# Attention over pairs of short batches: probabilities times values as four 256-column matmuls in place of three of 512

## The reference, cut to what matters

```python
qg = q.reshape(b, HKV, G, s, HD)                      # 8 groups of 4 heads
scores = jnp.einsum('bkgqd,bksd->bkgqs', qg, k) / math.sqrt(HD)
attn = jax.nn.softmax(scores + bias[None], axis=-1)    # causal, with a slope per head
out = jnp.einsum('bkgqs,bksd->bkgqd', attn, v)         # <- this product
out = out.reshape(b, H, s, HD).transpose(0, 2, 1, 3).reshape(b, s, H * HD)
```

## Time and profile before

| | |
|---|---|
| median of 3 runs | 2405.1 us (2403.43 to 2405.45) |
| the profiled execution's own time | 2406.15 us |
| its span | 2404.4 us |
| TensorE clock granted, mean | 0.999 of full |
| PE busy | 2378.0 us of the span, 11706 matmuls |
| DVE busy | 1725.5 us, 2770 instructions |
| ACT busy | 1325.7 us, 3273 instructions |
| HBM traffic | 131 GB/s over the span |

### The profile page before, as it was taken

One profiled execution on the slowest core, in us unless ns is written; L12 is line 12 of the kernel. 1 busy time (PEld: TensorE's weight loads), 2 busy tenths in 40 slices (PEclk: granted clock), 3 DMA queues, 4 the chain that ended last, 5 costly groups with the idle time before them and its releaser, 6 DMA issues.

```text
span 2404.4 us, 32917 instructions
## 1 busy us (share of the span) xinstructions
PE 2378.0 (99%) x11706; PEld 1979.4 (82%) x11706; DVE 1725.5 (72%) x2770; ACT 1325.7 (55%) x3273; POOL 246.3 (10%) x272
## 2 busy tenths in 40 slices
PE   8999999999999999999999999999999999999998
PEld 6887788888888888888888888888888888888887
DVE  6758878687836867777855777777874686868682
ACT  4245656566625656566724656565743565747561
POOL 0101010101101001010011101010111101010111
PEclk9999999999999999999999999999999999999999
DMA  7774544341542242423443242423254242423260
GB/s 252 261 288 150 171 140 149 134 155 57 191 142 88 85 140 77 141 79 130 135 157 114 71 158 71 158 71 123 88 177 140 71 150 79 140 89 127 69 208 36
DMA packets 88438, 316.15 MB, mean 131 GB/s; under 512 B 12716, under 2 KB 13228, under 8 KB 87124
## 3 DMA queue, kind: packets, MB, share of 16 engines
q1 hardware_dynamic: 70292, 247.14, 31.0%
q10 hardware_dynamic: 10944, 37.54, 4.2%
q0 software_dynamic: 7040, 29.36, 3.4%
HBM read 282.54 MB, written 31.46 MB: 131 GB/s over the span
## 4 chain that ended last, share of the span: by engine, by line
PE 94%; DVE 2%; DMA 2%; issue 1%; ACT 0%; ACTq 0%; POOL 0%; POOLq 0%; DVEq 0%
PE main L1008 80%; PE pv_bank L1202 3%; PE qt_bank L1167 3%; PE s_bank L1183 2%; PE s_bank L1184 2%; PE pt_bank L1191 1%; PE pt_bank L1008 1%; PE s_bank L1008 1%; PE qt_bank L1008 1%; DMA sums<-in_wo 1%; DVE ring L1483 1%; DMA t_scratch<-sums 1%; DVE setup L1483 0%; PE qt_bank L1104 0%; PE s_bank L1104 0%
## 5 line engine op out<-in xcount | busy, mean ns | idle before, releaser
L1008 PE MATMUL main<-ring,act_hi 128*128 128x512 f32 x3584 | 1147.9, 401 | 0.0
L1008 PEld LDWEIGHTS main<-ring,act_hi 128*128 128x128 f32 x3584 | 641.3, 189 | 111.2
L1008 PE MATMUL main<-ring,act_lo 128*128 128x512 f32 x1792 | 702.1, 392 | 0.0
L1008 PE MATMUL main<-ring,lefts 128*128 128x512 f32 x2688 | 624.5, 391 | 0.0
L1483 DVE TENSOR_TENSOR ring<-raw,ring 128x1024 fp32r<-128x1024 f32 x448 | 555.4, 1242 | 58.7 <-ACT ring L1213 57.1
L1008 PEld LDWEIGHTS main<-ring,lefts 128*128 128x128 f32 x2688 | 501.7, 188 | 103.1
L1213 ACT ACTIVATE ring<-raw 128x1024 fp32r<-128x1024 f32 x448 | 472.4, 1057 | 178.3 <-PE main L1008 165.8
L1008 PEld LDWEIGHTS main<-ring,act_lo 128*128 128x128 f32 x1792 | 336.5, 188 | 74.5
L1810 POOL TENSOR_TENSOR rstd<-mean,half 128x4 f32<-128x4 f32 (+1 forms) x192 | 173.9, 906 | 1617.9 <-DVE mean L1599 1617.9
L1369 ACT ACTIVATE prob<-score,peak 128x64 f32<-128x64 f32 x512 | 136.8, 338 | 159.7 <-DVE peak L1654 159.2
L1341 ACT ACTIVATE sq<-main 128x128 f32<-128x128 f32 x640 | 168.8, 277 | 73.3 <-PE main L1008 69.0
(11 more groups left out here) (146 smaller groups left out, 2353.6 us busy)
## 6 DMA issues: line engine op xcount, KB each, us to landing
raw<-in_wq SPq DMA_DIRECT2D x128, 512.0 KB, 4.0
raw<-t_scratch SPq DMA_DIRECT2D x128, 512.0 KB, 3.3
raw<-in_wo SPq DMA_DIRECT2D x96, 512.0 KB, 3.3
raw<-in_wkv SPq DMA_DIRECT2D x64, 512.0 KB, 3.9
sums<-in_wo ACTq DMA_DIRECT2D x32, 512.0 KB, 6.9
t_scratch<-sums ACTq DMA_DIRECT2D x32, 512.0 KB, 5.0
raw<-f_scratch SPq DMA_DIRECT2D x32, 512.0 KB, 5.4
acc<-in_x POOLq DMA_DIRECT2D x16, 512.0 KB, 3.6
```

The costliest lines, as they stand in the source:

```text
L1008: mm = eng.matmul(bank, a, b, start=start and n == 0 and m == 0, stop=stop and n == len(terms) - 1 and m == 2, skip_group_check=further)
```

## The change

The values are held in one tensor `values` in place of `v_hi` and `v_lo`, with the same bytes. For batch b it has the hi part on that batch's 64 partitions and the lo part on the other 64. `pt_hi` gets the batch's hi probabilities on both halves of the partitions, by a new ScalarE stage `p_twice` of two copies, directly behind `p_hi`. A matmul of `values` by `pt_hi` then sums hi x hi and lo x hi over the 128 rows, and one by `pt_lo`, still zero on the other half, adds hi x lo. Each covers one batch's 256 columns. To place the halves, `v_hi` becomes two copies and `v_lo` two subtractions of 64 partitions each, and `v_lo` crosses the halves.

```diff
         def transpose_p():
             self.fill("pt", "prob_t", (k,), "p_lo")
             self.at(base, when("tp_hi"), lambda: self.add("p_hi", k))
+            self.at(base, when("tp_hi"), lambda: self.add("p_twice", k))
             self.at(base, when("tp_lo"), lambda: self.add("p_lo", k))
...
-        v_hi = sb("v_hi", [P, TILES, 2, HD], F32R)
-        v_lo = sb("v_lo", [P, TILES, 2, HD], F32R)
+        values = sb("values", [P, TILES, 2, BPT, HD], F32R)
...
                 elif stage == "pv":
-                    w.wait_ge("p_hi", k)
+                    w.wait_ge("p_twice", k)
...
-                    for m, (a, p) in enumerate(((v_hi, pt_hi), (v_hi, pt_lo), (v_lo, pt_hi))):
-                        mm = eng.matmul(pv_bank[:, :, :].rearrange("p b n -> p (b n)"), a[:, t, g % 2, :],
-                                        p[:, :, :].rearrange("p b n -> p (b n)"), start=m == 0, stop=m == 2)
+                    for b in range(BPT):
+                        both = values[:, t, g % 2, b, :]
+                        eng.matmul(pv_bank[:, b, :], both, pt_hi[:, b, :], start=True, stop=False)
+                        mm = eng.matmul(pv_bank[:, b, :], both, pt_lo[:, b, :], start=False, stop=True)
...
-                    copy(v_hi[:, tile_of(k), :, :], norm_bank(k)[:, 2 * HD:4 * HD].rearrange("p (j n) -> p j n", j=2), "v_hi")
+                    for b in range(BPT):
+                        act = eng.activation(values[rows_of(b), tile_of(k), :, b, :], values_in(k, b), ACT.Copy)
+                    act.then_inc(done["v_hi"], 1)
...
+                elif stage == "p_twice":
+                    k, = key
+                    w.wait_ge("p_hi", k)
+                    for b in range(BPT):
+                        act = eng.activation(pt_hi[rows_of(1 - b), b, :], f32(pt_hi[rows_of(b), b, :]), ACT.Copy)
+                    act.then_inc(done["p_twice"], 1)
...
                 elif stage == "v_lo":
-                    low(v_lo[:, tile_of(k), :, :], norm_bank(k)[:, 2 * HD:4 * HD].rearrange("p (j n) -> p j n", j=2),
-                        v_hi[:, tile_of(k), :, :], stage, k)
+                    w.wait_ge("v_hi", k)
+                    for b in range(BPT):
+                        rest = eng.tensor_tensor(values[rows_of(1 - b), tile_of(k), :, b, :], values_in(k, b),
+                                                 f32(values[rows_of(b), tile_of(k), :, b, :]), ALU.subtract)
```

More of the change, by code:

```diff
@@ L797, in build_program @@
         bias_parts = k_flat.rearrange("p (u s n) -> p u s n", u=2, s=2)
-        enc_rows = [v_hi[:, :, :, :].rearrange("p a b n -> p (a b n)"), v_lo[:, :, :, :].rearrange("p a b n -> p (a b n)")]
-        enc_hi = v_hi[0:ENC, :, :, :].rearrange("p a b n -> p (a b n)")
-        enc_lo = v_lo[0:ENC, :, :, :].rearrange("p a b n -> p (a b n)")
+        v_flat = values[:, :, :, :, :].rearrange("p t g b n -> p (t g b n)")
+        enc_rows = [v_flat[:, 0:CHUNK], v_flat[:, CHUNK:2 * CHUNK]]
+        enc_hi, enc_lo = (part[0:ENC, :] for part in enc_rows)
         x_even = [lefts[:, 2, i, :, :, :].rearrange("p a h n -> p (a h n)") for i in range(2)]
@@ L900, in norm_bank, with values_in @@
             return bank_of("mm", k, 0)
+        def values_in(k, b):
+            return norm_bank(k)[rows_of(b), 2 * HD:4 * HD].rearrange("p (j n) -> p j n", j=2)
         def norm_width(k):
@@ L1602, in _ @@
                     w.wait_ge("square", k)
-                    low(v_lo[:, tile_of(k), :, :], norm_bank(k)[:, 2 * HD:4 * HD].rearrange("p (j n) -> p j n", j=2),
-                        v_hi[:, tile_of(k), :, :], stage, k)
+                    w.wait_ge("v_hi", k)
+                    for b in range(BPT):
+                        rest = eng.tensor_tensor(values[rows_of(1 - b), tile_of(k), :, b, :], values_in(k, b),
+                                                 f32(values[rows_of(b), tile_of(k), :, b, :]), ALU.subtract)
+                    rest.then_inc(done[stage], 1)
                 elif stage == "scale":
```

## The result

The changed kernel takes 2451.57 us (median of 5 runs, 2450.43 to 2451.70) against 2404.09 for the kernel before (5 runs in the same session). The ratio is 1.019, with a 95% interval of 1.0179 to 1.0202, so it is 47.5 us slower. The profiled execution took 2450.43 us, with a span of 2448.6.

The account below looks back on a forecast made before the run. The prediction took PE's stream, busy 2378.0 of 2404.4 us, as the bound. Waits of 50.8 us less 27 saved on matmuls gave +24, so 2429 us, 1.0% slower, with a range of 2408 to 2446.

Parts of the forecast that it names:

- Step A: Query step with four chunks to split: late squares make `query_t` wait 0.81 us, 28 times, 22.7 us.
- Step B: First step of a kv unit behind q units: `key_t` waits 0.9 us, 12 times, 10.7 us.
- Step C: Second step of a kv unit behind q units: 0.5 us more wait, 12 times, 6 us.
- Step D: Fourth step of every kv unit, 16 in all: already waits, and `v_hi`'s 0.51 us goes through, 8.2 us.
- the fourth pair: Fourth pair of q units in a block, leading into an output unit: estimated waits of 3.2 us in all.
- I take 0.77, and 0.03 for the wait: Added ACT time of `p_twice` per step: 0.77 us for two copies without overlap, plus 0.03 waiting on `p_hi`, 0.80.
- The matmuls, 27 us: `pv` on PE: four matmuls at 0.120 us replace three at 0.23, saving 0.21 a step, 27 us over 128 steps.
- Worse, 2450: Rival: 50 query steps that were charged nothing wait another 0.4 us too, 2450 us; chance 0.10.
- Covered copies: Rival: unseen slack hides the copies, `query_t` starts without a wait, 2380 us; chance 0.14.
- Cheap copies: Rival: the two `p_twice` copies overlap, 0.6 us a pair, 2417 us; chance 0.18.
- About the same: Rival: margins grow again in half the tight query steps, waits of 27 us balance the saving, 2405 us; chance 0.08.
- The matmuls save nothing: Rival: with 0.19 us a start four `pv` matmuls cost 0.76, more than 0.69, 2465 us; chance under 0.02.

Follow-up runs that it names:

- e9: The changed kernel with only the first of the two `p_twice` copies, the second left out: 2420.74 us, ratio 1.0066.
- e4: The changed kernel with `p_twice` moved behind the squares and the first ring copy: 2423.19 us, ratio 1.0072.
- e1: The kernel before with its product as four matmuls of 256 columns and no new copies: 2386.68 us, ratio 0.9916.
- e2: The kernel before with its three matmuls kept and `p_twice` alone added behind `p_hi`: 2430.61 us, ratio 1.0098.
- e3: The kernel before with only `v_hi` and `v_lo` made in 64-row halves: 2418.69 us, ratio 1.0050.
- e5: The kernel before with four matmuls of 256 columns and `p_twice`, but the values not split: 2419.19 us, ratio 1.0058.
- e17: The product of e12, with value copies moved and mean, `scale`, `gain` ahead of long DVE pieces in second to fourth key steps: 2383.03 us, ratio 0.9909.
- e6: The changed kernel with `p_twice` reading a constant from SBUF, so without its wait on `p_hi`: 2442.43 us, ratio 1.0149.
- e11: The changed kernel with the values' high half copied instead of the probabilities, and their low half in 64-row matmuls: 2519.23 us, ratio 1.0475.
- e13: e12 with `scale`, `gain` and `v_lo` of the fourth key step directly behind the mean on DVE: 2421.02 us, ratio 1.0064.
- e12: e11 with its two 64-row matmuls made full-height and no wait between matmuls: 2442.83 us, ratio 1.0149.

## Why the prediction came out short

The direction, the places and the saving were right. The size was not: waits rose by 67 us and not by 51, by the table above. The 16 us between are 2.7 in step A, 4.3 in B, 2.6 in C, 4.4 in D and 2.2 in the fourth pair. Two steps of the sum failed: the 0.80 us that `p_twice` was to cost (A, B and C), and the `v_lo` that was charged with nothing in D.

- **"I take 0.77, and 0.03 for the wait", so 0.80.** This step failed, and it measured 0.99. The pair takes 0.84, since a copy from SBUF takes 416 ns and one from PSUM 379, and the squares start 0.87 behind its start. Then the first accumulator read starts 0.29 behind its square (34.92 - 34.63), 0.12 later than the 0.17 to 0.18 with one copy (e9) or with the copies behind (e4). No term of the sum held that. By the overlap rule of the Trainium skill ("ScalarE: Activation LUTs", "What ACT_TABLE_LOAD costs") the pair would take less. Here it does not overlap: two copies of 416 ns take 0.84 us.
- **Step A, 0.81 forecast, 0.96 measured.** The mean comes 3.38 behind `prob_t` in place of 3.20, which is the 0.09 of the copies and 0.09 of the squares. The two steps of the first block that waited before grew by 0.18 each, and not by 0.81, which takes 1.3 us off the total.
- **Step B, 0.9 forecast, 1.2 measured.** From `p_twice` to the mean it is 2.45, where the forecast makes 2.24. `v_lo` starts 0.03 behind the mean's end and so does what follows it, which adds 0.1. The first such step of the kernel adds 1.95 in place of 0.9.
- **Step C, 0.5 forecast, 0.7 measured above the waits of before.** The mean comes 0.42 later behind the start of `pv` and not 0.19. From there to the transposes it is 0.11 more, as forecast.
- **Step D, 0.51 forecast, 0.79 measured.** The forecast let only `v_hi`'s 0.51 through and put `v_lo`'s 0.43 at nothing, because ACT's ring copy was what DVE waited for. The ring piece starts 2.55 behind `v_hi` (96.83 - 94.28), and before it was 1.88, so 0.67 go through, and `v_lo` ends last. From the ring piece to the transposes it is another 0.13 (2.20 for 2.07).
- **The matmuls, 27 us.** Measured 26. Rows at 0.120 were the right price.
- **The fourth pair of q units, 3.2 forecast, 5.4 measured,** most of it `prob_t`. The forecast called this an estimate, and which of its waits it had wrong was not taken apart.
- **What no term held.** 67 less 26 is 41, and the span grew by 44. The rest is seen in the first transposes behind a wait, 0.165 apart in place of 0.109. The medians differ by 3 more, because the profiled run of before was 2.1 over its median and that of after 1.1 under it.

"Worse, 2450" has the time but not its mechanism: of the query steps charged with nothing two lose 0.07 each, and the others nothing. "Covered copies" fell at its own point of decision, since `query_t` waits in A. "Cheap copies" fell by the 0.84. "About the same" fell because all 28 steps A wait. "The matmuls save nothing" fell by the starts 0.12 apart and by e1.

That the copies and the split cause it is shown by e2, e3, e5 and e9, and that the product does not, by e1 and e17. Why the first read comes late is open. It is not the wait (e6), it needs both copies (e9), and it is in time where the copies stand behind (e4).

## What to carry to other kernels

Price added work by the queue that it lengthens: find the narrowest chain behind it and follow it in absolute times to the instruction that the bounding engine waits for. Parts that look cheap alone add up to more together when they share a margin (17 against 47 us here), so a forecast should sum them at the place, not each by itself. When reordering only moves the waits, look for a form of the product that needs the copy at the side with fewer steps, and then put the short chain ahead of long pieces in each queue.

## What was not expected of the hardware

- 64-row matmuls between 128-row ones, with a wait between the two of 64 rows, make a product of 1.05 us from one of 0.48 (e11).
- With two `p_hi` and two `p_twice` copies ahead of the squares, the first accumulator read starts 0.29 behind its square. With two copies of `p_hi` alone (before) and with three copies (e9) it is 0.17. Step D, where the squares stand directly behind two 64-row copies too, has 0.17 in the changed kernel as well, so a pair of 64-row copies alone does not make it.
- On ACT, a 64-row copy of 256 columns takes 416 ns from SBUF and 379 from PSUM.
- In e13 to e17, `scale` starts 0.81 us of idle time behind the mean, while `rstd` runs 0.70 on GpSimd. With a ring piece between the two on DVE (e11, e12) it starts some 0.6 behind that piece instead, so the piece covers nothing. `rstd` itself takes about 1.7 in 12 of the 16 fourth steps of e12, beside the ring piece, and 0.70 otherwise.
- In e12 seven stretches of some 3.5 us have a granted clock of about half (0.51, 1.2 GHz) that begins in or shortly behind a wait of PE, as of 2.2 us in a step D. They cost some 8 us beside the waits.
